# Moving the last third of the probabilities' low halves from VectorE to GpSimd

## What is computed

```python
h = _L0_tok_ref(x, ...)                       # three-level Haar transform, gated bands, inverse
h = h + _L0_attn_ref(_layernorm(h), ...)      # 16 heads of 16, causal, 256 tokens of width 256
h = h + _L0_ffn_ref(_layernorm(h), ...)       # 16 experts, each takes its 32 best tokens of an image
```

```python
scores = (jnp.einsum('bqhd,bkhd->bhqk', q, k) + mask) * inv_scale
attn = jax.nn.softmax(scores, axis=-1)
out = jnp.einsum('bhqk,bkhd->bqhd', attn, v)
```

## Time and profile before

| | |
|---|---|
| median of 3 runs | 1222.81 us (1219.66 to 1225.08) |
| the profiled execution's own time | 1221.32 us |
| its span | 1219.5 us |
| busy in the span | PE 941.7, DVE 731.6, POOL 674.6, ACT 575.0 us |
| low halves by POOL (line 451) | 128, 157.3 us busy |
| low halves by DVE (line 875) | 64, 49.6 us busy |

### The profile page before, as it was taken

One profiled execution on the slowest core, in us unless ns is written; L12 is line 12 of the kernel. 1 busy time (PEld: TensorE's weight loads), 2 busy tenths in 40 slices (PEclk: granted clock), 3 DMA queues, 4 the chain that ended last, 5 costly groups with the idle time before them and its releaser, 6 DMA issues.

```text
span 1219.5 us, 18959 instructions
## 1 busy us (share of the span) xinstructions
PE 941.7 (77%) x6870; PEld 808.8 (66%) x6870; DVE 731.6 (60%) x1598; ACT 575.0 (47%) x1065; POOL 674.6 (55%) x582
## 2 busy tenths in 40 slices
PE   0000037798888888888628999999999999999996
PEld 0000026677677767765417888888888888888885
DVE  5999525688888888886473544454444344544441
ACT  1000011477777777778513444455445444544442
POOL 2455251366666566666333666666656565765654
PEclk9999997899999999998668999999999999999998
DMA  7222319966887788661222554555554545555433
GB/s 197 79 95 73 106 48 157 134 105 141 137 135 132 135 131 139 125 97 37 83 67 76 93 102 109 113 105 105 110 112 85 106 109 117 99 105 111 84 52 35
DMA packets 105950, 127.60 MB, mean 105 GB/s; under 512 B 12288, under 2 KB 92160, under 8 KB 104832
## 3 DMA queue, kind: packets, MB, share of 16 engines
q1 hardware_dynamic: 81280, 92.81, 35.2%
q0 software_dynamic: 24576, 33.57, 16.9%
HBM read 79.67 MB, written 46.14 MB: 103 GB/s over the span
## 4 chain that ended last, share of the span: by engine, by line
PE 47%; DVE 2%; POOL 1%; issue 1%; DMA 0%; ACT 0%; POOLq 0%; ACTq 0%
PE y_ps L1092 15%; PE gate_ps L1078 15%; PE value_ps L1078 14%; PE xT_ps L1059 2%; DVE top_index L1232 1%; DVE top L1226 1%; DVE work L1234 0%; PE gate_ps L1101 0%; POOL out L1034 0%; POOL x_rows L1023 0%; DMA x_rows<-normed_scratch,slot_row 0%; DMA rw2s<-in_L_ffn_router_w 0%; ACT xg_hi L1125 0%; DVE L L1224 0%; DVE rw_shifted L1216 0%
## 5 line engine op out<-in xcount | busy, mean ns | idle before, releaser
L1034 POOL DMA_INDIRECT out<-y_rows,slot_row x128 | 203.0, 1586 | 192.6 <-ACT y_rows L1138 163.1
L1201 DVE TENSOR_TENSOR hidden<-silu_g,value_ps 128x512 f32<-128x512 f32 x128 | 88.0, 688 | 306.4 <-PE value_ps L1078 171.3
L451 POOL TENSOR_TENSOR probs_k<-probs_full,probs_k 128x512 f16<-128x512 f32 x128 | 157.3, 1230 | 137.8 <-ACT probs_k L720 133.9
L1146 ACT ACTIVATE silu_g<-gate_ps 128x512 f32<-128x512 f32 x128 | 76.7, 599 | 276.9 <-PE gate_ps L1078 276.9
L1023 POOL DMA_INDIRECT x_rows<-normed_scratch,slot_row x128 | 146.7, 1146 | 56.7 <-issue 38.7
L713 ACT ACTIVATE probs_full<-scoresT_ps,log 128x512 f32<-128x512 f32 x192 | 132.2, 689 | 92.2 <-PE scoresT_ps L593 47.0
L1092 PE MATMUL y_ps<-w_hi,hidden_lo 128*128 128x256 f32 x512 | 145.0, 283 | 0.0
L1092 PE MATMUL y_ps<-w_lo,hidden_hi 128*128 128x256 f32 x512 | 145.0, 283 | 0.0
L1092 PE MATMUL y_ps<-w_hi,hidden_hi 128*128 128x256 f32 x512 | 144.8, 283 | 0.0
L720 ACT ACTIVATE probs_k<-probs_full 128x512 f16<-128x512 f32 x192 | 120.3, 627 | 0.0
L1078 PE MATMUL gate_ps<-xg_hi,w_hi 128*128 128x512 f32 x256 | 103.6, 405 | 2.1 <-ACT xg_hi L1125 2.1
(11 more groups left out here) (199 smaller groups left out, 2333.4 us busy)
## 6 DMA issues: line engine op xcount, KB each, us to landing
w_raw<-in_L_ffn_w SPq DMA_DIRECT2D x48, 512.0 KB, 4.0
q_stack<-q_scratch SPq DMA_DIRECT2D x96, 128.0 KB, 5.0
k_stack<-k_scratch SPq DMA_DIRECT2D x96, 128.0 KB, 8.0
x_tile<-in_x SPq DMA_DIRECT2D x4, 1024.0 KB, 7.1
h_scratch<-rec_tile SPq DMA_DIRECT2D x4, 1024.0 KB, 4.3
hacc<-h_scratch SPq DMA_DIRECT2D x4, 1024.0 KB, 5.5
q_scratch<-q_hi SPq DMA_DIRECT2D x16, 256.0 KB, 2.2
q_scratch<-q_lo SPq DMA_DIRECT2D x16, 256.0 KB, 2.5
```

The lines of the kernel that those rows point to most:

```text
L451: G.tensor_tensor(probs(b, 1, n), pf[N % 3][:].rearrange("p (a q) -> p a q", a=4 if n % 3 == 2 else 2), probs(b, 0, n), ALU.subtract).then ...
L1034: G.indirect_dma_start(out=rows, out_offset=bass.IndirectOffsetOnAxis(ap=idx[:, col:col + 1], axis=0), in_=ys[c][:, j, :], in_offset=None, ...
L1146: A.activation(sg[ft % 2][:], GP[ft % 2][:], ACT.Silu).then_inc(silu_done, 1)
L1201: V.tensor_tensor(hf[ft % 2][:], sg[ft % 2][:], VP[ft % 2][:], ALU.mult).then_inc(hf_done, 1)
```

## The change

`probs_lo` no longer returns early, so POOL makes all twelve low halves of an image, each in the iteration of its own `probs_hi`. For n % 3 == 2 it raises `pc_done`, as DVE did. DVE's block of lines 872 to 876 goes. Nothing else is touched: buffers, offsets and the waits of ACT and PE are as they were.

```diff
             def probs_lo(b, n):
                 N = NB * b + n
-                if n % 3 == 2:
-                    return
                 g.wait_ge(pa_done, N + 1)
                 G.tensor_tensor(probs(b, 1, n), pf[N % 3][:].rearrange("p (a q) -> p a q", a=4 if n % 3 == 2 else 2),
-                                probs(b, 0, n), ALU.subtract).then_inc(pb_done, 1)
+                                probs(b, 0, n), ALU.subtract).then_inc(pc_done if n % 3 == 2 else pb_done, 1)
...
                 if b >= 0 and r % 3 == 0:
                     outputs(b, r // 3)
-                b, r = due(t, EX + 2)
-                if b >= 0 and r % 3 == 2:
-                    v.wait_ge(pa_done, NB * b + r + 1)
-                    V.tensor_tensor(probs(b, 1, r), pf[2][:].rearrange("p (a q) -> p a q", a=4), probs(b, 0, r),
-                                    ALU.subtract).then_inc(pc_done, 1)
```

## The result

The changed kernel takes 1210.9 us (median of 4 runs, 1208.92 to 1211.76) where the kernel before, run beside it on the same chip, takes 1222.93: a ratio of 0.9902 with a 95% interval of 0.9876 to 0.9927. That is 12.0 us off; the forecast was 6.6. The kernel is faster by more than 0.5%. Two executions that took 1394.57 us (the changed kernel with SP's copies moved) and 1494.25 us (the kernel before) are slow ones and stand outside every time and ratio given here. The changed kernel's profiled execution took 1208.92 us, with a span of 1207.0 against 1219.5 before.

What follows compares the result with a forecast made beforehand. No engine was full; a closed loop of waits over ACT, POOL, DVE and PE set 24.02 us per image. 13.05 + 7.96 + 2.22 = 23.23, nine images 7.1 off, last low half 0.5 lost: 1216.2 us, range 1209 to 1227.

Steps and rivals of the forecast that it cites:

- The closed loop: Attention stage's chain of waits, exp 6 to the next image's exp 6: 24.02 us per image, forecast to become 23.23.
- way: From ACT's exp 6 to DVE's use of the second rstd power: 12.53 us before, forecast 13.05 on POOL's queue.
- middle: From DVE's use of the power to its v_sum: 9.27 us before, forecast 7.96.
- back: From v_sum through PE's transposes and scores to the next image's exp 6: 2.22 us, forecast unchanged.
- the second normalise: DVE's second normalise instruction, due 0.08 to 0.18 us before POOL's lo 1 asks: DVE wins, saving 0.89 us.
- PE's floor: PE's late scores of step 2 hold DVE's maximum, so the middle takes 7.96 us instead of DVE's own 7.26.
- The last low half: Final lo, on the path to the experts: takes 1.16 us on POOL instead of 0.64, 0.5 lost.
- PE waits 2.7 us there for a copy of the maxima: After 502 us, where projections run out: this wait covers a later lo, so the change there is nought.
- DVE still loses the normalise: Rival, chance 0.27: the pair takes 1.63 us again, period 23.98, time 1223 us, within 0.5%.
- More blocks: Rival, chance 0.18: POOL's los block both layernorms' normalise pairs; with three lost races period 25.20, 1234 us, slower.
- No floor: Rival, chance 0.10: step 2's scores run ahead on PE, middle 7.26, period 22.53, time 1210 us, faster.
- The likeliest case: The forecast itself, chance 0.45: period 23.23 us, time 1216.2 us, own range 1213 to 1220.

Runs made afterwards that it cites:

- the run with the clear ahead of it: Changed kernel plus a 128-column PSUM clear (0.17 us) on DVE, once just ahead of the normalise pair's step: 1217.36 us in a single execution.
- the run with the copies moved: Kernel before, with SP's copies into k_stack moved behind the copies of the maxima: 1214.6 us, ratio 0.9935.
- the kernel with the add moved: Kernel before with low halves 2, 5 and 11 on POOL, 8 on DVE, and POOL's hacc add moved behind low half 6: 1211.1 us, ratio 0.9903.

## Why the prediction was right and wrong

**What held.** The closed loop exp 6, power, v_sum, exp 6 sets the period, and its terms did what the sum says, with the sign of each: way 12.95 us (forecast 13.05), middle 7.85 (7.96), back 2.17 (2.22). Each of the four low halves has its place, as the table shows. DVE won the second normalise by a lead of 0.11 us, inside the 0.08 to 0.18 foreseen, and the run with the clear ahead of it shows what losing costs. PE's floor is there: DVE idles 0.53 us ahead of its maximum of step 2. The last low half cost 0.45, forecast 0.5.

**The sizes.** All three parts were forecast a little too long: the way by 0.10, since v_rest and the hacc add took 404.37 - 402.02 = 2.35 instead of 2.50, with 0.03 given back between low halves 6 and 8; the floor by 0.11; the way back by 0.05. The period is 22.95 instead of 23.23, 0.28 less, and with nine images that is 2.5 of the 5.9 us of span that were missing (12.5 measured, 6.6 forecast). The forecast lay at its bound of 0.5%, so small terms decided on which side it fell.

**The step that failed** is "PE waits 2.7 us there for a copy of the maxima, which covers a later lo: nought too". A wait for a copy was taken for a cushion of fixed place. In fact it is a race between the copy and PE, and in the kernel before it cost more than its length, with PE's clock falling behind it: 3.5 us, by the run with the copies moved. In its first profile the changed kernel lost 1.5 us one image earlier and did not have the 3.5: 2.0 net. In its second, PE waited 1.1 us for the copy, its clock was low for longer, and the net was 42.31 - 42.13 = 0.2: about the nought of the forecast, but as the sum of a loss and a gain, not by cover. That PE comes later there and so can find the copy done is read from the traces; what the wait costs is shown by the run, in one profile of each kernel. So the term can't be one number, while the shorter period stands in both profiles. The 0.6 us up to 297 us, also taken at nought, and the 0.5 in the experts' stage I have not taken apart.

**The rivals.** That DVE still loses the normalise is refuted, pair 0.75. More blocks: refuted for the changed kernel; the kernel with the clear ahead, where the pair of the other layernorm met low half 2 as well (1.17 us), shows how near it was. No floor: refuted by the 0.53. The likeliest case came true, but its own range, 1213 to 1220, did not hold 1210.9; the full one did, by the part of it that was laid there for the case without floor, so that is luck.

**The rule of the skill.** Low half 0 starts at 414.94 and lasts 1.17 us, to 416.11, and DVE's first normalise starts at 415.83, 0.89 after it, with the pair of usual length. So the Trainium skill's rule (SBUF — State Buffer, Who interferes with whom), by which the port pair is held for the whole instruction, does not hold to the recorded end of POOL's instruction here. That the two exclude each other, that the first to come wins and that the loser waits, the trace bears out, with 0.75 against 1.65 us for the pair.

## What to carry to other kernels

Ask of each moved instruction what it stands ahead of on its old queue and on its new one: of four equal ones, two were worth 0.54 and 0.86 us per image, and of the other two, the one that had stood ahead of idle time should have stayed. Where a loop closes over several engines, lay out its way term by term, and look for pairs that exclude each other within a tenth of a microsecond: such a race is worth more than the instruction that is moved. Don't price a wait in an image outside the pattern at nought, and reckon with what PE's idle time does to its clock.

## What the runs showed of the hardware that was not expected

- An instruction of 0.17 us on DVE cost 0.85 us per image, by losing one race with POOL by 0.03 us and then meeting POOL again in the next pair. In the kernel with the add moved, POOL lost a race by the same 0.03 us, and its instruction took 1.63 us instead of 1.21.
- POOL's low half of 1.17 us let DVE's normalise start 0.89 us after its own start.
- After 2.35 to 2.7 us of idle time, PE's granted clock fell to between 0.50 and 0.82 in the 5 to 9 us that followed, in the kernel before and in the changed one, for a longer time in one execution of the changed kernel than in the other. It also fell in the midst of steady images, in which the image before ran at 1.00 (ahead of the fall PE was busy 2.38 of 3.5 us with 28 instructions, one image earlier 2.37 with 28); such a slip makes one image 1.5 us longer. What sets it off there is open.
